# First cross attention: the product with the values turned round, its operands split in two

## The reference

```
x:   8 x 64 x 512 (8 sequences of 64 tokens)    ctx_1024: 8 x 1601 x 256
q = layernorm(x) Wq, k = y Wk, v = y Wv         16 heads of 32, q and k normed in each head
ctx = softmax(q k / sqrt(32)) v                 over the first 1585 keys of each sequence
x = x + (ctx + a second attention over the last 16 keys) Wo + bo
```

## Time and profile before

| | |
|---|---|
| time, median of 3 runs | 2759.47 us (2752.17 to 2764.41) |
| profiled execution | 2750.2 us, span 2747.5 us |
| PE busy | 2434.7 us (89%) |
| DVE, ACT, POOL busy | 63%, 42%, 36% |
| mean granted TensorE clock | 0.939 of full |
| stage x0b, first scores to last strip added | about 141 to 976 us |

### The profile page before, as it was taken

How to read it: one execution, slowest core, us unless ns; L and a number is a source line. 1 busy time by engine, 2 the same in 40 slices (tenths; PEclk the granted TensorE clock), 3 DMA queues, 4 the chain that set the end, 5 groups by cost and what they waited for, 6 DMA issues and landing times. The chain is left out here.

```text
span 2747.5 us, 40047 instructions
## 1 busy us (share of the span) xinstructions
PE 2434.7 (89%) x12756; PEld 2003.8 (73%) x12756; DVE 1719.2 (63%) x2728; ACT 1155.4 (42%) x2084; POOL 1002.0 (36%) x688
## 2 busy tenths in 40 slices
PE   4699999999999969998898899999999997788744
PEld 2588888888888748886676678888888876566632
DVE  3457766766767723333443278888788884666677
ACT  1344444443444313332221367666676662332211
POOL 3147667667667610000011035544555460110000
PEclk9699999999999979998899899999999999899957
DMA  3000000000000012210231200000000002110010
GB/s 103 1 25 25 25 1 25 25 1 25 19 7 1 1 64 69 68 61 17 68 86 37 83 25 25 16 18 17 26 25 16 10 1 76 52 41 31 12 62 16
DMA packets 104256, 89.51 MB, mean 33 GB/s; under 512 B 32752, under 2 KB 82432, under 8 KB 104080
## 3 DMA queue, kind: packets, MB, share of 16 engines
q1 hardware_dynamic: 103792, 87.28, 10.5%
q0 software_dynamic: 288, 0.00, 0.0%
HBM read 86.22 MB, written 1.05 MB: 32 GB/s over the span
## 5 line engine op out<-in xcount | busy, mean ns | idle before, releaser
L2184 POOL TENSOR_TENSOR xT<-xT,x1b_ring 128x512 f32<-128x512 f32 (+1 forms) x176 | 248.3, 1411 | 213.4 <-ACT x1b_ring L2314 206.7
L869 POOL TENSOR_TENSOR x0b_krstd<-x0b_krstd,minus_half 128x24 f32<-128x24 f32 x64 | 267.0, 4173 | 108.7 <-DVE x0b_krstd L933 87.9
L889 POOL TENSOR_TENSOR xT<-xT,x0b_ring 128x512 f32<-128x512 f32 (+1 forms) x176 | 243.8, 1385 | 142.4 <-ACT x0b_ring L1078 130.6
L983 DVE TENSOR_TENSOR x0b_ring<-x_ps,x0b_krstd 128x512 f32<-128x512 f32 (+1 forms) x208 | 143.0, 688 | 134.4 <-PE x_ps L828 132.2
L111 DVE TENSOR_TENSOR x1b_plo<-x1b_ring,x1b_phi 128x512 fp32r<-128x512 f32 (+1 forms) x208 | 222.2, 1068 | 6.6 <-issue 4.9
L854 PE MATMUL x_ps<-x0b_ring,x0b_vn 128*128 128x256 f32 (+1 forms) x832 | 217.5, 386 | 1.8 <-ACT x0b_ring L1078 1.6
L828 PE MATMUL x_ps<-x0b_qbd,x0b_kT 128*128 128x256 f32 (+1 forms) x832 | 217.6, 384 | 1.6 <-DVE x0b_ring L983 1.4
L1078 ACT ACTIVATE x0b_ring<-x0b_ring 128x512 f32<-128x512 f32 (+1 forms) x208 | 130.7, 630 | 207.7 <-DVE x0b_ring L961 197.3
L2329 ACT ACTIVATE x1b_ring<-x_ps,x1b_keymask 128x512 f32<-128x512 f32 (+1 forms) x208 | 143.1, 688 | 131.3 <-DVE xT L2256 126.0
L116 PE MATMUL x_ps<-x1b_qy,x1b_yT 128*128 128x512 f32 (+1 forms) x416 | 175.8, 423 | 4.3 <-ACT x1b_ring L2329 2.9
L828 PEld LDWEIGHTS x_ps<-x0b_qbd,x0b_kT 128*128 128x128 f32 (+1 forms) x832 | 149.9, 187 | 30.1 <-issue 6.4
(11 more groups left out here) (575 smaller groups left out, 5844.5 us busy)
## 6 DMA issues: line engine op xcount, KB each, us to landing
x_y<-in_ctx_dram SPq DMA_DIRECT2D x8, 1536.0 KB
x_y<-in_ctx_dram SPq DMA_DIRECT2D x24, 512.0 KB, 3.8
a_wn<-in_L_attn_W_Q_dram SPq DMA_DIRECT2D x16, 256.0 KB, 3.1
a_wn<-in_L_attn_W_K_dram SPq DMA_DIRECT2D x16, 256.0 KB, 3.5
a_wn<-in_L_attn_W_V_dram SPq DMA_DIRECT2D x16, 256.0 KB, 4.1
a_won<-in_L_attn_W_O_dram SPq DMA_DIRECT2D x16, 256.0 KB, 2.9
x1a_wq<-in_L_xattn_Wq_dram SPq DMA_DIRECT2D x4, 1024.0 KB, 10.7
x1c_wo<-in_L_xattn_Wo_dram SPq DMA_DIRECT2D x8, 512.0 KB, 6.9
```

The source lines that it names most:

```text
L869: ins = g_.tensor_tensor(r, r, c.minus_half[:, 0:8].unsqueeze(1).broadcast_to([P, whole, 8]), ALU.pow)
L889: g_.tensor_tensor(total[half][0:m, :], old, src, ALU.add).then_inc(summed, 1)
L983: v.tensor_tensor(slot.rearrange("p (h s) -> p h s", s=S), ps[0:m, S_BANK + n % 2, :].rearrange("p (h s) -> p h s", s=S), spread(krstd[0:m ...
L2184: g_.tensor_tensor(total[half][0:m, :], old, src, ALU.add).then_inc(summed, 1)
```

## The change

The product is turned round. The exponentials become the stationary operand and the values move. Each tile's exponentials are split: ACT copies them to float32r (`p_high`, one tile after the exponential), and POOL subtracts (`p_low`, one tile later). The values are split too, and between their halves stand two columns of ones, so that one product gives the values' sum, and the sum of the exponentials. For each pair of heads (four in a tile) there are two products: high with 130 columns (64 high, 2 ones, 64 low), and low with 66. The tile's product now comes 17 steps behind the scores, and ahead of `make` in a step.

The running sum on POOL goes, with its transposes and reduces on PE and DVE. The split of V's second half is new on DVE; the inverse deviations are made one key tile at a time on POOL, six steps ahead. The copy out of PSUM moves from point 29 to point 30, and the normalization to 31, on one column per head. A new entry T, two transposes, turns each half's result back, at step 6 and step 19 of the next round, and DVE adds it. Some tiles move into xn and xT to make room.

```diff
-        LIFE, LAG_SUB, LAG_PV = 17, 14, 16
+        LIFE, LAG_SUB, LAG_HI, LAG_LO, LAG_PV, RSTD_AHEAD = 17, 14, 15, 16, 17, 6
...
-        S_BANK, O_BANK, M_BANK, X_BANK, KV_BANKS = 0, 2, 4, 7, (3, 5, 6)
+        S_BANK, O_BANK, M_BANK, KV_BANKS = 0, 2, 4, (5, 6, 7)
...
+        PAST = entries("6:T0 19:T1")
...
 # PE, in a step: the sums' transposes go, and make comes after the product
-                    for ahead, e in made_at(part, n):
-                        make(at, seq + ahead, (ahead, *e))
...
-                        pe.wait_ge(exp_done, TILES * seq + (t + 1))
+                        pe.wait_ge(p_done, TILES * seq + (t + 1))
...
                         if kt == 0 and not (part == "first" and t == 0):
                             pe.wait_ge(out_kept, 2 * seq + t // KT)
-                        for g in range(2):
-                            mm = pe.matmul(ps[:, O_BANK, g * GC:(g + 1) * GC], vn[0:m, kt, half, g * P:(g + 1) * P],
-                                           ring[0:m, key_slot(par, t, LIFE), g * GC:(g + 1) * GC],
-                                           start=(kt == 0 and g == 0), stop=(kt == KT - 1), skip_group_check=True)
+                        for i in range(4):
+                            hi, lo = (a[0:m, i * P:(i + 1) * P] for a in (p_high[(t + TILES * par) % 4], p_low[t % 2]))
+                            col = (i % 2) * (VW + VD)
+                            values = vn[0:m, kt, 4 * half + i, :]
+                            pe.matmul(ps[:, O_BANK + i // 2, col:col + VW + VD], hi, values,
+                                      start=(kt == 0 and i % 2 == 0), stop=False, skip_group_check=True)
+                            mm = pe.matmul(ps[:, O_BANK + i // 2, col:col + VW], lo, values[:, 0:VW],
+                                           start=False, stop=(kt == KT - 1), skip_group_check=True)
                         mm.then_inc(pv_done, 1)
+
+                    for ahead, e in made_at(part, n):
+                        make(at, seq + ahead, (ahead, *e))
...
 # POOL, in a step
+                        if not (part == "first" and t < 2):
+                            g_.wait_ge(pv_done, TILES * seq + (t - 1))
+                        g_.wait_ge(p_hi, TILES * seq + (t + 1))
+                        split(g_, p_high[(t + TILES * par) % 4][0:m, :], p_low[t % 2][0:m, :],
+                              ring[0:m, key_slot(par, t, LIFE), :]).then_inc(p_done, 1)
+                    if n + RSTD_AHEAD < TILES:
+                        deviation(seq, n + RSTD_AHEAD)
...
 # DVE, in take
+                    if e[1] == "V":
+                        v.wait_ge(v_hi, KT * seq + (kt + 1))
+                        split(v, vn[0:m, kt, :, 0:VD], vn[0:m, kt, :, VW:VW + VD],
+                              ps[0:m, bank, :].rearrange("p (h d) -> p h d", d=VD)).then_inc(v_done, 1)
...
 # ACT, at the head of a step
-                    f = half_at(part, n, 29)
+                    f = half_at(part, n, 30)
...
+                        act.activation(osb[:, :, :].rearrange("p (k i) n -> p k (i n)", k=2), products, ACT.Copy
+                                       ).then_inc(out_kept, 1)
+                    t = lagged(part, n, LAG_HI)
+                    if t is not None:
+                        act.wait_ge(exp_done, TILES * seq + (t + 1))
+                        act.activation(p_high[(t + TILES * par) % 4][0:m, :], ring[0:m, key_slot(par, t, LIFE), :], ACT.Copy
+                                       ).then_inc(p_hi, 1)
```

More of the change, by code:

```diff
@@ L650, in x0_main_attention @@
         headkn = st.sb("headkn", [P, 4])
[L651 removed]
         rowmax = st.sb("rowmax", [P, 2, 4])
[L653 to L654 removed]
+        inverse = st.sb("inverse", [P, 4])
+        osb = spare[:, 0:4 * (VW + VD)].rearrange("p (i n) -> p i n", i=4)
+        onew = spare[:, 528:528 + 4 * VD].rearrange("p (i n) -> p i n", i=4)
+        krstd = spare[:, 784:784 + 2 * KT * 8].rearrange("p (s t h) -> p s t h", s=2, t=KT)
         run = [c.xT[:, f, :] for f in range(2)]
[L656 to L658 removed]
+        p_high = [st.sb(f"phi{i}", [P, COLS], F32R) for i in range(4)]
+        p_low = [st.sb(f"plo{i}", [P, COLS], F32R) for i in range(2)]
+        S_BANK, O_BANK, M_BANK, KV_BANKS = 0, 2, 4, (5, 6, 7)
+        products = ps[:, O_BANK:O_BANK + 2, 0:2 * (VW + VD)]
         size = lambda kt: P if kt < FULL else TAIL0
@@ L675, in x0_main_attention @@
                         "22:K020 23:K021 24:W02 24:Y30 25:Y31")
+        PAST = entries("6:T0 19:T1")
+        LAST = entries("32:T0 45:T1")
+        STEPS = TILES + 20
         def made_at(part, n):
+            past = [] if part == "first" else PAST.get(n, [])
+            here = HERE.get(n, []) + (LAST.get(n, []) if part == "last" else [])
             ahead = [] if part == "last" else AHEAD.get(n, [])
-            return [(0, e) for e in HERE.get(n, [])] + [(1, e) for e in ahead]
+            return [(-1, e) for e in past] + [(0, e) for e in here] + [(1, e) for e in ahead]
         BEFORE = [(1, *e) for n in sorted(AHEAD) for e in AHEAD[n]]
@@ L688, in x0_main_attention @@
             for kind, rel in batches:
-                for e in (BEFORE if kind == "before" else [(a, *e) for n in range(TILES) for a, e in made_at(kind, n)]):
+                for e in (BEFORE if kind == "before" else [(a, *e) for n in range(STEPS) for a, e in made_at(kind, n)]):
                     sched.add((rel, *e), KV_BANKS[uses % len(KV_BANKS)])
@@ L719, in steps @@
                         step("body", ("body", i, rel), 2 * i + (1 + rel), 1 - rel, n)
-            for n in range(TILES + 18):
+            for n in range(STEPS):
                 step("last", ("last", ITERATIONS, 0), B - 1, (B - 1) % 2, n)
@@ L773, in make @@
                         return
+                    if kind == "T":
+                        pe.wait_ge(normed, 3 * (2 * seq + e[2]) + 3)
+                        for g in range(2):
+                            mm = pe.transpose(out[:, g * P:(g + 1) * P], onew[:, 2 * g:2 * g + 2, :].rearrange("p k n -> p (k n)"), c.ident[:, :])
                     if kind == "V":
@@ L894, in _, with deviation @@
-                steps(g_, lambda e: deviations(0, e[2], e[3]) if e[1] == "W" else None, step)
+                def deviation(seq, n):
+                    half, kt = n // KT, n % KT
+                    if kt in (0, 3, 6, 9):
+                        g_.wait_ge(w_done, 8 * seq + (4 * half + kt // 3 + 1))
+                        g_.sem_inc(apart, 1)
+                    r = krstd[0:size(kt), half, kt, :]
+                    g_.tensor_tensor(r, r, c.minus_half[0:size(kt), 0:8], ALU.pow).then_inc(rstd_done, 1)
@@ L896, in _ @@
+                for n in range(RSTD_AHEAD):
+                    deviation(0, n)
+                steps(g_, lambda e: None, step)
             @block.vector
@@ L926, in take @@
                         v.wait_ge(y_done, 8 * seq + (2 * q + ch + 1))
+                        v.sem_inc(kv_free[bank], 1)
+                    if e[1] == "V":
+                        _, _, kt = e
+                        m = size(kt)
+                        v.wait_ge(v_hi, KT * seq + (kt + 1))
+                        split(v, vn[0:m, kt, :, 0:VD], vn[0:m, kt, :, VW:VW + VD],
+                              ps[0:m, bank, :].rearrange("p (h d) -> p h d", d=VD)).then_inc(v_done, 1)
+                        v.wait_ge(v_done, KT * seq + (kt + 1))
+                        v.sem_inc(kv_free[bank], 1)
+                    if e[1] == "T":
+                        _, _, f = e
+                        v.wait_ge(kv_full[bank], nth + 1)
+                        v.sem_inc(apart, 1)
+                        for j in range(4):
+                            rows = slice(32 * j, 32 * j + 32)
+                            o = ctxT[rows, 2 * f:2 * f + 2, bass.ds(seq * S, S)]
+                            new = ps[rows, bank, 0:2 * P].rearrange("p (g h n) -> p g h n", g=2, h=2)[:, :, j % 2, :]
+                            ins = v.tensor_tensor(o, new, o, ALU.add)
+                        ins.then_inc(added, 1)
+                        v.wait_ge(added, 2 * seq + (f + 1))
                         v.sem_inc(kv_free[bank], 1)
```

126 lines of the change are left out of this document (38 added, 88 removed).

## The result

The changed kernel takes **2805.27 us** (median of 4 runs, 2796.03 to 2808.95) against 2756.2 us (2752.17 to 2764.41) of the kernel before, measured beside it: a ratio of **1.0172 [1.0146, 1.0198]**, 49 us slower. The forecast was 2782, +23. The profiled execution took 2808.95 us, span 2806.8.

The account below looks back on a forecast made before the run. PE was taken to bound the stage, busy 98 of 100 us at full clock. 6 - 10 + 17 + 8 + 0 + 2 = +23 us gave 2782 us; the sum's own range was 2768 to 2805, the full range 2728 to 2825.

Parts of the forecast that it names:

- a product at +27: Upper bound of the new product on PE: 0.99 us a tile if 17 ns a product come on top of the load.
- POOL's +20: Rival: POOL becomes the bound in the light steps, +20 us on top, about 2798 us; 14%.
- The product, +6: New product on PE: eight products paced by their loads, 0.89 us a tile against 0.86; +6 us, bounds -6 and +27.
- the faster rival: New product on PE: load and matmul pairs pace at 0.08 us, -44 us in place of +6, 2732 us; 14%.
- The rival of a float32 pace: New product on PE: short float32r products run at the float32 pace, +95 us in place of +6, 2871 us; 15%.
- The sums' transposes, -10: PE: four L808 and four L814 go per half and two T come, 12 fewer transposes a sequence; -10 us.
- The copy wait, +17: Steps 4 and 17 and the end: PE's product waits for ACT's copy out of PSUM; +17 us, bounds 0 and +26.
- The rival that the new waits do not show: PE's waits: ACT reaches the copy before K100 and K000 are taken; 2757 to 2765 us, no change; 22%.
- The wait at step 14, +8: Row maximum's spread on PE: V8 delays Y00's split, so the wait grows from 0.56 to about 1.5 us; +8 us, bounds 0 and +12.
- POOL, 0: POOL: split replaces running sum at 1.40 us, power 1.63 a tile; the light steps' shortfall of 0.8 us is absorbed; 0.
- The end, +2: Stage end after the last scores: the split of 13 tiles ends about 2 us later, the rest takes as long; +2 us.
- the step that failed is the first: Stage's bound: PE busy 98 of 100 us at the full granted clock, 2.4 GHz, so its microseconds count in full.

Follow-up runs that it names:

- Edit 5: Changed kernel with the low product streaming two columns, the ones alone, in place of 66: 2814.26 us, 1.022 to the kernel before.
- edit 1: Changed kernel with ACT's copy out of PSUM moved to point 29, ahead of the step's key copies: 2813.25 us, 1.0211 to the kernel before.
- Edit 8: Kernel before with only the order changed, its own product ahead of the step's projections: 2769.37 us, 1.0067.
- edit 4: Changed kernel with Y00 and Y01 moved from steps 12 and 13 to 13 and 14: 2801.95 us, 1.0179 to the kernel before.
- edits 9 and 10: Last half's product widened to 256 columns: 9 on the make-first, 130-column-low kernel, with Y00 and Y01 later, 2750.82 us; 10 on the changed kernel, 2808.04 us.
- edit 3: Changed kernel with make ahead of the product again and V's entries one step later: 2774.9 us, 1.0096 to the kernel before.

## Why the prediction was right, and where it was wrong

The direction was right, and the time lies in the range; the increase was forecast at +23 and is +49. That the range holds it is in part luck: 2805 lies at the top of the prediction's own narrower range (2768 to 2805, whose top the terms at half weight do not give: they come to about 2797), and the room above was kept for a product at +27 and for POOL's +20, and neither came. By its own steps:

- **The product, +6.** Right: 0.11 us a pair, 0.89 a tile. Edit 5 shows that columns up to 66 are free. The Trainium skill's 81 ns for a pair (TensorE: Matmul & The Clock Gate, Back-to-back issue gap) is not reached in this stream: 111 ns in the profile after. With it falls the faster rival. The rival of a float32 pace falls too.
- **The sums' transposes, -10.** Right. The four L808 stood behind the products of steps 1 and 14, which are 0.41 and 0.40 us shorter, and the four L814 behind those of steps 2 and 15, 0.66 and 0.76 shorter; T takes 0.44 back. That is 14 us in eight sequences. All of PE's full-clock work is 7 us less, against a forecast of -4 for both terms.
- **The copy wait, +17.** Right in place, cause and count: 15 times, up to 1.2 us. It sums to 12.3 by the profile: at step 17 it is the full 1.17, and at step 4, where the clock is often at half, PE arrives later and waits less. At the full clock steps 4 and 17 are 1.44 longer each. But the conclusion one would draw, that removing it gives 12 to 17 us, failed in edit 1. The rival that the new waits do not show falls.
- **The wait at step 14, +8.** Right in kind. The list of waits has +5.3 us, and step 13, which it ends, is 1.44 longer at the full clock, 11.5 in eight, inside the bounds of 0 to 12. Edit 8 has 0.86 of it from the order alone, and edit 4 takes 0.6 off by moving Y00 and Y01: the chain through Y00 is seen, and the rest of it is argued.
- **POOL, 0.** Right: PE waited for its split twice, 1.0 us in all. It was costed too cheaply, at 1.63 us for eight columns against a mean of 1.82, with 1.33 for the split.
- **The end, +2.** Too small, and the smaller part of the matter. From the last scores on the stage takes 40.5 us for 36.4, +4. But the six steps ahead, 19 to 24 of the last sequence, take 22.8 for 12.9. The last 60 us of the stage run at a clock of 0.50; their clock entry is 26.8 us against 3.4 before. Not all of it is the price of the end: edits 9 and 10 gave back 8 to 10 us of clock there, and 3 and 7 us of length.
- **In no term.** Steps 0, 3, 16, 21 and 22 are 1.74 us a sequence longer at the full clock, 14 us in eight. What makes them so was not followed.
- **The clock.** This is the largest missing term, and the step that failed is the first: "a microsecond taken from PE's work, or added to it, counts in full", at the granted clock of the earlier trace rows. That clock of 1.00 was read as a property of the stage, where it hangs on what PE streams as well. Over the stage the clock took 9.5 us before and 63.9 after by the books; by the count of steps it is worth some 28 of the 63, an estimate. The busy share gave no sign of it: from 500 to 700 us PE is busy 96 of 100 before and 93 after, and twelve falls come with PE busy throughout.

What the runs show and what they leave open. Shown: order and width each carry a part of the loss, and together all of it. Undoing the order gives 39 us with the wide low product and 30 without (21 by the ratios). Widening the low product gives 21 us with make first; alone it gives 12, or 4 by the ratios, which is not clear of noise. Both together give 51 (46 by the ratios). Shown: for the same body, wider streams bring the clock cost from 64 to 32 to 15 us, with the mean clock of all executions rising in step, though they add work. Shown: taking PE's waits away does not bring the clock back (edits 1 and 3), and twelve falls come without a wait. Not shown: what starts a fall without a wait at steps 3 and 15, each within a step of W's sixteen matmuls (widening W in the changed kernel would test it, and was not run); why 2 columns cost so little more clock than 66; what the clock by itself is worth, between 28 and 54 of the 63 us. Single profiled executions of one kernel differ by some us in this column, so only its large differences are used.

## What to carry to other kernels

When a product is turned so that short moving operands follow a load each, price it twice: by the pace of the loads, and by what the granted clock does in the stretches that it fills. A wait found and priced right is not yet a gain to be had: here PE, freed of it, ran at a lower clock. Try its removal together with whatever holds the clock. When the loads set the pace anyway, columns up to the load's own time are free (66 in place of 2 here), and may pay for themselves in clock. Look at what PE did ahead of each fall of the clock, for one behind a wait and one in full work ask for different mends. And ask of every reordering which engine's chain it delays: putting the product ahead of the projections cost the unchanged kernel 17 us with no other edit.

## What the runs showed that was not expected

- TensorE's granted clock fell to 0.50 for a whole stretch of 60 us while PE was busy 53.64 of 60 us (1.2 GHz for 2.4), and in edit 3 for 20 us with PE busy all 20. Kernels with a wider end had 0.84 and 0.93 in their last 20 us, with less busy time.
- Twelve times in the changed kernel the clock fell with no idle time of PE in the 7 us before. In the kernel before the two falls between 200 and 900 us came at the end of waits of over 5 us.
- Streaming more made a kernel faster: 256 columns in place of 130 and 66 added 18 us of work to the stage and took 49 us of clock off it, 16 us in the median (12 by the ratios).
- Removing a wait of 12 us lowered the mean clock of the execution from 0.922 to 0.911 in the profiled ones (0.922 to 0.925 against 0.911 to 0.919 in all), and the time did not fall.
- POOL's power of 128x8 took 1818 ns in the mean of 208 (16 of them 49x8) where 24 columns had taken 4173: cut in three, it costs 1.3 times as much.
